# A fused FFN on one core: stationary operands of the routed tiles moved off 16-byte lines

## What is computed

```python
w = weights[subjects]; b = bias[subjects]
h = jnp.einsum('bct,bcd->bdt', x, w) + b[:, :, None]          # 64 x 64 x 512, as 4096 tokens
scores = sigmoid(h @ gate_weight.T)                           # 16 experts
# 2 of 4 groups by their two best biased scores, then 4 experts; weights normed, times 2.5
def body(acc, inp):                                           # each of the 16 experts
    g, u, d, we = inp
    y = silu(h @ g.T) * (h @ u.T) @ d.T                       # 512 -> 256 -> 512
    return acc + we[:, None] * y, None
shared = silu(h @ shared_gate.T) * (h @ shared_up.T) @ shared_down.T
x = x + out + shared
```

## Time and profile before

| what | value |
|---|---|
| median of three runs | 826.39 us (825.04 to 826.95) |
| the profiled execution's own time | 826.33 us |
| its span, first to last instruction | 824.5 us |
| mean granted TensorE clock | 0.998 of 2.4 GHz |
| TensorE matmul busy | 812.5 us |
| TensorE weight loads busy | 649.7 us |
| VectorE busy | 485.0 us |
| ScalarE busy | 388.3 us |
| GpSimd busy | 433.4 us |

### The profile page before, as it was taken

How to read it: one execution, slowest core, us unless ns; L and a number is a source line. 1 busy time by engine, 2 the same in 40 slices (tenths; PEclk the granted TensorE clock), 3 DMA queues, 4 the chain that set the end, 5 groups by cost and what they waited for, 6 DMA issues and landing times.

```text
span 824.5 us, 19365 instructions
## 1 busy us (share of the span) xinstructions
PE 812.5 (99%) x4133; PEld 649.7 (79%) x4134; DVE 485.0 (59%) x1017; ACT 388.3 (47%) x782; POOL 433.4 (53%) x399
## 2 busy tenths in 40 slices
PE   9999999999999999999999999999999999999996
PEld 5578778888887888888888888888888888888874
DVE  5798899627444446644457446647557466464441
ACT  4864334535334345534455445546455355453441
POOL 5403112625567555566665665655565573765543
PEclk9999999999999999999999999999999999999999
DMA  8986969899999899899997999899998998998965
GB/s 288 394 332 177 247 149 260 204 203 268 239 251 237 177 192 176 202 276 241 182 196 185 270 216 217 210 267 189 229 266 175 282 246 198 236 206 164 198 94 68
DMA packets 145305, 181.52 MB, mean 220 GB/s; under 512 B 30570, under 2 KB 103922, under 8 KB 142834
## 3 DMA queue, kind: packets, MB, share of 16 engines
q0 software_dynamic: 37776, 89.08, 52.3%
q1 hardware_dynamic: 106528, 80.45, 38.4%
q10 hardware_dynamic: 834, 10.49, 3.6%
HBM read 82.52 MB, written 67.17 MB: 182 GB/s over the span
## 4 chain that ended last, share of the span: by engine, by line
PE 93%; DVE 3%; issue 1%; DMA 1%; ACT 1%; POOLq 0%; POOL 0%; DVEq 0%; SPq 0%; ACTq 0%
PE psGU L1111 47%; PE psY L1111 23%; PE psY L1169 5%; PE psH L982 4%; PE psGU L1152 3%; PE psGU L1154 3%; PE psGU L1153 3%; PE psT L982 1%; DMA raw_w<-ffn_w 1%; PE psY L1031 1%; PE psGU L1031 1%; PE psH L1008 1%; PE psM L1139 1%; PE psM L968 0%; DVE aT_low L1703 0%
## 5 line engine op out<-in xcount | busy, mean ns | idle before, releaser
L1111 PE MATMUL psGU<-split_w,xT_pair 128*128 x1716 | 415.9, 391 | 1.0 <-issue 1.0
L1111 PEld LDWEIGHTS psGU<-split_w,xT_pair 128*128 128x128 f32 x1716 | 321.9, 188 | 71.7 <-issue 1.9
L694 POOL DMA_INDIRECT out<-y_ring,idx_all x143 | 228.8, 1600 | 203.6 <-SPq L583 184.1
L1758 DVE SCALAR_TENSOR_TENSOR aT<-aT,w_ring,psGU 128x256 f32<-128x256 f32 x143 | 68.6, 480 | 238.6 <-ACT aT L934 216.1
L689 POOL DMA_INDIRECT tok_ring<-h_rows,idx_all x143 | 150.3, 1051 | 73.3 <-issue 42.0
L1111 PE MATMUL psY<-split_w,hidT_hi 128*128 x564 | 187.9, 414 | 0.0
L934 ACT ACTIVATE aT<-psGU 128x256 f32<-128x256 f32 x143 | 55.0, 384 | 255.2 <-PE psGU L1111 255.2
L840 ACT ACTIVATE y_ring<-psY 128x512 f32<-128x512 f32 x173 | 103.6, 599 | 101.1 <-PE psY L1111 63.3
L1111 PE MATMUL psY<-split_w,hidT_lo 128*128 x282 | 111.4, 395 | 0.0
L1111 PEld LDWEIGHTS psY<-split_w,hidT_hi 128*128 128x128 f32 x564 | 95.4, 189 | 13.5 <-issue 0.2
L1743 DVE STREAM_TRANSPOSE psT<-x_ring 128x512 f32<-128x512 f32 x143 | 102.5, 717 | 0.1
(11 more groups left out here) (268 smaller groups left out, 651.4 us busy)
## 6 DMA issues: line engine op xcount, KB each, us to landing
x_ring<-tok_ring SPq DMA_DIRECT2D x284, 128.0 KB
raw_w<-ffn_w SPq DMA_DIRECT2D x17, 1536.0 KB, 10.1
out<-y_ring POOLq DMA_DIRECT2D x32, 256.0 KB, 7.5
x_ring<-x_pairs SPq DMA_DIRECT2D x12, 512.0 KB, 8.6
h_rows<-tok_ring SPq DMA_DIRECT2D x16, 256.0 KB, 9.7
h_rows<-y_ring SPq DMA_DIRECT2D x16, 256.0 KB, 10.0
tok_ring<-h_rows,idx_all POOLq DMA_INDIRECT x143, 6.5
out<-y_ring,idx_all POOLq DMA_INDIRECT x143, 6.2
```

The costliest lines, as they stand in the source:

```text
L694: pool.indirect_dma_start(out[:, :], bass.IndirectOffsetOnAxis(idx_all[:, r:r + 1], 0), y_ring[:, r % YRING, :], None, compute_op=ALU.add) ...
L1111: mm = pe.matmul(dst, a[:, slot, c], w(at + col + k * H), start=(k == 0 and a is high and at == 0), stop=(k == parts - 1 and a is low))
L1758: v.scalar_tensor_tensor(out=hid[:, half, :], in0=gate, scalar=w_ring[:, w_slot, bass.ds(expert, 1)], in1=up, op0=ALU.mult, op1=ALU.mult). ...
```

## The change

The eight buffers become views into one buffer, `stationary`. Rows of the four inputs lie 513 words apart and rows of the four hidden parts 257 words apart, so that `xT_hi` of even and odd tiles and `xT_lo` of even and odd tiles begin 0, 4, 8 and 12 bytes off a multiple of 16 bytes, and the hidden parts in the same way. The buffer is 1,024 bytes longer than the three that it replaces, and the buffers behind it move by as much. The shared part's code takes the hidden operands as two halves, since the two halves no longer lie next to each other. Each engine has the same instructions in the same order as before; the loops, semaphores and counts are the same.

```diff
         aT = sb("aT", [P, 2, H])
-        xT_pair = sb("xT_pair", [P, GROUP, H], F32R)
+        stationary = sb("stationary", [P, GROUP * H + P + GROUP * I + P], F32R)
+        xT_pair = stationary[:, 0:GROUP * (H + 1)].rearrange("p (t h) -> p t h", h=H + 1)[:, :, 0:H]
         xT_hi, xT_lo = xT_pair[:, 0:2, :], xT_pair[:, 2:4, :]
         silu, hid = aT[:, :, 0:I], aT[:, :, I:2 * I]
-        hidT_hi = sb("hidT_hi", [P, 2, I], F32R)
-        hidT_lo = sb("hidT_lo", [P, 2, I], F32R)
+        hidT_at = GROUP * H + P
+        hidT = stationary[:, hidT_at:hidT_at + GROUP * (I + 1)].rearrange("p (t i) -> p t i", i=I + 1)[:, :, 0:I]
+        hidT_hi, hidT_lo = hidT[:, 0:2, :], hidT[:, 2:4, :]
...
             if c == 1:
-                return hidT_lo[:].rearrange("p a i -> p (a i)")
+                return hidT_lo
             if g % 2 == 0:
-                return hidT_hi[:].rearrange("p a i -> p (a i)")
-            return tok_high[:, H:2 * H] if g == 1 else ties_low[:, H:2 * H]
+                return hidT_hi
+            return in_halves(tok_high[:, H:2 * H] if g == 1 else ties_low[:, H:2 * H])
+
+        def in_halves(ap):
+            return ap.rearrange("p (a i) -> p a i", a=2)
...
-                token = slice(j * P, (j + 1) * P)
+                pair, half = divmod(j, 2)
+                token = slice(half * P, (half + 1) * P)
                 for c in range(IK):
-                    low = shared_hid_low(g, c)
+                    low = in_halves(shared_hid_low(g, c))
                     for a, at in ((shared_hid_high(g, c), 0), (shared_hid_high(g, c), EW), (low, 0)):
                         w = at + UP + c * H
-                        mm = pe.matmul(psY[n % 2][:], a[:, token], split_w[:, w:w + H], start=(c == 0 and a is not low and at == 0),
+                        mm = pe.matmul(psY[n % 2][:], a[:, pair, token], split_w[:, w:w + H], start=(c == 0 and a is not low and at == 0),
                                        stop=(c == IK - 1 and a is low))
```

More of the change, by code:

```diff
@@ L432, in group_high @@
             if g % 2 == 0:
-                return xT_pair[:]
+                return xT_pair
             if g < NT // GROUP - 1:
@@ L856, in shared_hid_highs @@
                 act.wait_ge(hid_ready, GROUP * g + 2 * c + 2)
-                act.activation(shared_hid_high(g, c), shared_hid(g, c), ACT.Copy).then_inc(hidhi_ready, 2)
+                act.activation(shared_hid_high(g, c), in_halves(shared_hid(g, c)), ACT.Copy).then_inc(hidhi_ready, 2)
             def shared_y(g, j):
@@ L1702, in split_shared_hid @@
                 hid_c = shared_hid(g, c)
-                v.tensor_tensor(shared_hid_low(g, c), hid_c, shared_hid_high(g, c).bitcast(F32), ALU.subtract
-                                ).then_inc(hidT_ready, 2)
+                v.tensor_tensor(in_halves(shared_hid_low(g, c)), in_halves(hid_c), shared_hid_high(g, c).bitcast(F32),
+                                ALU.subtract).then_inc(hidT_ready, 2)
             def shared_step(n):
```

## The result

The changed kernel takes 832.54 us (median of 7 runs, 831.75 to 835.39) against 826.59 us for the one before in the same comparison: a ratio of **1.0086** (95% interval 1.0069 to 1.0102), slower by 6 us between the medians and by 7 us by the ratio. The profiled execution has 833.56 us, with a span of 831.8 us against 824.5 us. 832.5 us lies in the range of 823 to 834.5 us, but the forecast itself, no change, was wrong; it had 0.60, slower 0.26. That the range held the result is luck: its upper end was drawn to take in rival 1 with its 834.2 us, and what rival 1 says did not happen.

A forecast was written before the change was run, and what follows sets the result against it. The prediction took TensorE alone to bound the kernel, busy 99% of the span. Its terms, 0 + 0 + 0 + 0, left the time unchanged at 826.4 us, with an 8-in-10 range of 823 to 834.5 us.

The forecast's parts named there:

- rival 1: An off-line weight load takes twice its time, paid only where no matmul covers it: +7.8 us, 834.2 us; chance 0.10.
- What bounds the kernel: Whole kernel: nothing beside TensorE sets the time, with 812.5 us of matmul in a span of 824.5 us.
- The price of the load itself: Routed tiles' weight loads: a load's occupation, 0.11 us, does not grow with the offset; taken as 0, upper bound 7.8 us.
- the bare load: First down-product load behind a tile's transposes, not covered by a matmul; off a line in the 71 odd tiles.
- What a load takes from the matmul beside it: Routed matmuls: slowing of the running matmul by 1,710 off-line loads; taken as 0, bounded by ±26.8 us.
- The 0.0157 us: Routed matmuls: the 38 cycles above one column per cycle in each 0.229 us, which no row names.
- rival 4: Moving pieces or writers 2 to 5 us slower (0.07); or 0.002 us less per routed matmul, up to 5 us faster (0.05).
- The shared part: Shared gate, up and down products: off-line moving pieces and 80 off-line stationary operands, all taken as 0.
- the moving pieces: Shared gate and up products: three of four 128-column input pieces begin off a line; at most 5 ns each, 0.68 us.
- The writers and the buffers behind: ScalarE and VectorE writes of high and low parts, any slowdown hidden, and buffers 1,024 bytes further on: both 0.
- Rival 2: Routed matmuls: line reads of the load take 0.0157 us from the moving stream and straddling doubles them: 861 us; chance 0.08.
- rival 3: Routed matmuls: the excess is load and stream colliding at equal places within a line; moved, they miss: -26.8 us, 799.6 us; chance 0.08.

## Why the prediction was right or wrong

**What bounds the kernel: right.** TensorE set the time before and sets it after; the 7.3 us of span are 7.0 us of its busy time, and no wait was added.

**The price of the load itself: right.** I took 0 from line 1091 against line 976, and expected loads of 186 to 192 ns. They are the same in every kernel of this study, wherever the operand begins (186 to 195 ns at the extremes, with a median of 187 or 188). Rival 1 falls with this: the second down matmul behind the transposes starts 319 instead of 314 ns after the first in odd tiles, 0.4 us in all and not 7.8 us, and the kernel with only the hidden parts padded, which has the bare load, is no slower.

**What a load takes from the matmul beside it: this step failed.** "I take 0, since loads of input and hidden part, on lines 1111 and 1169, all last 188 ns at the median or mean, and no row ties the excess to where an operand lies." The rows could not tie it, since all operands of the kernel began at the same place modulo 512 bytes: the trace held one point of the curve, and I read it as a flat curve. The price is not zero. The open term was bounded by ±26.8 us; it measured +5.4 us, 3 ns for each of 1,710 loads if it is put on them. But that is not what the price follows: operands all on a 16-byte line pay as much (836.6 and 834.1 us), and the hidden parts off a line hardly do (827.1 us). What the runs show in its place is a pace set by the difference between the starts of load and stream, 227.2 ns without one and 230.5 to 233.6 ns with one. The 0.0157 us from which I took the bound was a mean that holds unsettled matmuls as well: the settled pace of the routed part is 226.7 ns, as in the shared part, so the 0.002 us of rival 4 lies in the unsettled ones, and no kernel here took it out.

**The shared part: 0 was wrong, the bound nearly right.** For the moving pieces I had at most 5 ns each and 0.68 us; 7.4 ns and 0.9 us came, and 0.4 us more on the down matmuls, which I had at 0 as well. Line 1069, which I called nearest, streams 143 plain fp32 columns in 121 to 126 ns, almost twice the time per column, and did not carry over.

**The writers and the buffers behind: right,** at 0; the rows of the four writers are the same within 2 ns, and the kernel with only the hidden parts padded has the shifted buffers and no loss.

**The rivals.** Rival 2's 861 us and rival 3's 799.6 us both took the excess as a thing of loads that goes or doubles as a whole, and neither did. Both were right that the place of the load can cost the matmul beside it; rival 3 had the sign reversed, since load and stream that begin at the same place are the fast pair. Rival 4 came nearest in size, 2 to 5 us slower with 0.07 where 6 to 7 came, but named the moving pieces and the writers; the first of the two carries 0.9 us of it. "I am wrong if the distance of two matmuls on line 1111 depends on the slot" was the right test: 232.3 against 231.4 ns, and 4,406 against 4,381 ns for the tile.

**The two pages of the Trainium skill.** The experiments set how far each goes here. The line penalty that the Trainium skill states on its page SBUF — State Buffer, Specifications (TRN2), does not show in a load's duration (188 ns), and rows on 16-byte lines were as slow as rows off them; it fits only the stream that begins 4 bytes off, at 238.2 instead of 227.2 ns a matmul. The statement of the Trainium skill's page TensorE: Matmul & The Clock Gate, Part 2, that the next load takes no read bandwidth from the running matmul, would make 0 of the whole term. The measurement decides against that 0: with nothing changed in the routed product but where the load begins, the pace of the matmuls goes from 227.2 to 232.2 ns (4 bytes) or 233.4 ns (16 bytes). Whether it is read bandwidth that the load takes, no run shows.

## What to carry to other kernels

When TensorE is full of fp32r matmuls like these, each of 512 columns with a load of its own, keep the first bytes of stationary and moving operands equal modulo 256 bytes, and the moving one on a 16-byte line. Here, rows of 512 words in buffers placed one behind the other did so without being asked; a pad of 1, 4, 8 or 16 words a row, or a shift by 1, 4 or 32 words, undid it, while a pad of 64 words did not. A trace in which every operand has the same alignment cannot price another alignment; the term is then open in both directions, and a flat reading deserves less than 0.6. Judge it by the distance between starts, since the loads last 188 ns throughout.

## What was not expected of the hardware

- The pace of back-to-back matmuls of 512 fp32r columns depends on the difference between the starts of load and stream: a mean of 227.2 ns where it is 0 modulo 256 bytes (also when all is moved by 32 bytes, and with 256, 512 and 768 bytes), and 232.2, 233.4 and 232.4 ns at a constant 4, 16 and 128 bytes. Where the roles are exchanged, in the shared part, moving the stream alone by 16 bytes costs as well (226.4 to 230.4 ns). That the two reads meet in the memory would explain it; this is argued, not shown, and why 256 bytes is open.
- With both operands 4 bytes off a line the pace is regular but 234 to 240 ns, and the kernel 2.6% slower. With a stream 4 bytes off, group means are 236 to 242 ns wherever the load begins. Why one word costs it 11 ns of 227 is open too.
- The pace needs about ten matmuls behind two transposes to settle at 226.7 ns. Six down and four gate and up matmuls run unsettled, at 224 to 236 ns, in every clean kernel; the identity's place is not the cause; what is was not found.
- Of constant differences only 0, 4, 16 and 128 bytes were tried. Whether another one is faster than 0 stays open.
